# Key chunks of P.V in pairs in TensorE's order, in a fused attention and mixture-of-experts kernel

## What is computed

```python
q, k, v = (jnp.einsum('bsd,hdk->bhsk', x, w) for w in (w_q, w_k, w_v))   # x: 8 x 512 x 128, 16 heads of 64
weights = jax.nn.softmax(jnp.einsum('bhqk,bhmk->bhqm', q, k) / 8, axis=-1)
z = jnp.einsum('bhqm,bhmk->bhqk', weights, v)
z = jnp.einsum('bse,ed->bsd', jnp.transpose(z, (0, 2, 1, 3)).reshape(b, s, h * dk), w_o)
x = layernorm(x + (x + z))
combine = ...          # softmax over the top 2 of 8 experts of x @ gate_w, 0 for the others
h = jax.nn.silu(jnp.einsum('bsd,edf->ebsf', x, w1))
y = jnp.einsum('ebsf,efd->ebsd', h, w2)
x = layernorm(x + (x + jnp.einsum('ebsd,bse->bsd', y, combine)))
```

## Time and profile before

| | |
|---|---|
| median of 3 runs | 1282.63 us (1282.48 to 1285.91) |
| span of the profiled execution, first to last instruction | 1280.0 us |
| its own time: span and 2.6 us around it, by the median | about 1282.6 us |
| PE busy | 1196.7 us, 93% |
| DVE busy | 987.7 us, 77% |
| POOL, ACT busy | 679.6 us (53%), 602.0 us (47%) |

### The profile page before, as it was taken

How to read it: one execution, slowest core, us unless ns; L and a number is a source line. 1 busy time by engine, 2 the same in 40 slices (tenths; PEclk the granted TensorE clock), 3 DMA queues, 4 the chain that set the end, 5 groups by cost and what they waited for, 6 DMA issues and landing times. The chain is left out here.

```text
span 1280.0 us, 20247 instructions
## 1 busy us (share of the span) xinstructions
PE 1196.7 (93%) x4952; PEld 693.9 (54%) x4952; DVE 987.7 (77%) x1618; ACT 602.0 (47%) x744; POOL 679.6 (53%) x502
## 2 busy tenths in 40 slices
PE   5799999999999999999999999999998788888886
PEld 3454555555555555555555555555553566666664
DVE  4586888788888788888788888788887667777764
ACT  4444444444444444444444444444443555556553
POOL 0464644455544455544555544555546366666665
PEclk9898999999999999999999999999999889999999
DMA  9666666566665565665666665656660000000000
GB/s 213 162 161 153 157 155 157 144 156 147 157 156 140 144 155 146 158 159 153 150 150 153 159 148 140 150 149 152 160 161 21 21 9 17 17 17 16 8 9 17
DMA packets 91643, 153.47 MB, mean 120 GB/s; under 512 B 18016, under 2 KB 36960, under 8 KB 91616
## 3 DMA queue, kind: packets, MB, share of 16 engines
q1 hardware_dynamic: 91616, 153.14, 48.1%
HBM read 6.30 MB, written 2.10 MB: 7 GB/s over the span
## 5 line engine op out<-in xcount | busy, mean ns | idle before, releaser
L1025 DVE TENSOR_REDUCE neg_max<-psum 128x1 fp32r<-128x512 f32 x512 | 345.1, 680 | 114.1 <-PE psum L530 112.1
L1040 DVE RECIPROCAL zT<-zT 128x128 f32<-128x128 f32 x256 | 241.4, 944 | 4.2 <-ACT zT L865 2.2
L530 PE MATMUL psum<-k_stack,q_stack 128*128 128x512 f32 x512 | 224.6, 451 | 6.8 <-DVE neg_max L1025 1.4
L555 PE MATMUL psum<-q_stack,k_stack 128*128 128x512 f32 x512 | 210.5, 411 | 9.9 <-DMA q_stack<-q_stack 7.4
L858 ACT ACTIVATE probs_even<-psum 128x1024 f32<-128x1024 f32 x128 | 131.0, 1023 | 179.1 <-PE psum L556 179.1
L556 PE MATMUL psum<-q_stack,k_stack 65*128 65x512 f32 x512 | 205.2, 401 | 0.0
L396 POOL TENSOR_TENSOR probs_sum<-probs_even 128x512 f32<-128x512 f32 x64 | 82.5, 1289 | 227.4 <-PE psum L581 187.2
L396 POOL TENSOR_TENSOR probs_sum<-x_tok 128x512 f32<-128x512 f32 x64 | 82.2, 1284 | 226.9 <-PE psum L581 226.9
L530 PEld LDWEIGHTS psum<-k_stack,q_stack 128*128 128x128 f32 x512 | 97.1, 190 | 185.0 <-DVE neg_max L1025 87.9
L396 POOL TENSOR_TENSOR probs_sum<-probs_sum,probs_even 128x512 f32<-128x512 f32 x128 | 164.1, 1282 | 14.5 <-ACT probs_even L858 3.3
L396 POOL TENSOR_TENSOR probs_sum<-probs_sum,x_tok 128x512 f32<-128x512 f32 x128 | 164.3, 1283 | 11.3
(11 more groups left out here) (119 smaller groups left out, 1927.1 us busy)
## 6 DMA issues: line engine op xcount, KB each, us to landing
q_stack<-q_pair SPq DMA_DIRECT2D x128, 256.0 KB, 3.0
k_stack<-k_pair SPq DMA_DIRECT2D x128, 256.0 KB, 3.6
q_stack<-q_pair SPq DMA_DIRECT2D x128, 128.0 KB, 3.5
k_stack<-k_pair SPq DMA_DIRECT2D x128, 128.0 KB, 3.4
xT_cur<-xT SPq DMA_DIRECT2D x32, 512.0 KB, 3.0
wqk_cur<-w_tab SPq DMA_DIRECT2D x63, 256.0 KB, 3.3
wo_cur<-w_tab SPq DMA_DIRECT2D x64, 128.0 KB, 3.0
x_tok<-L_attn_x_dram SPq DMA_DIRECT2D x8, 256.0 KB, 5.4
```

Of the source, the lines that this page charges most:

```text
L530: nc.tensor.matmul(psum[:, COARSE + t % 2, :], q_stack[j][:, h, 0, t * P:(t + 1) * P], k_stack[j][:, h, 0, :], start=True, stop=True).then ...
L555: nc.tensor.matmul(psum[:, t, :], k_stack[j][:, h, 0, keys], q_stack[j][:, h, 0, :], start=True, stop=False)
L1025: nc.vector.tensor_reduce(neg_max[h][:, t:t + 1], psum[:, COARSE + t % 2, :], AX.X, ALU.max, negate=True).then_inc(s["max_done"], 1)
L1040: nc.vector.reciprocal(zT[:, cols], zT[:, cols]).then_inc(s["r_done"], 1)
```

## The change

In TensorE's body, P.V chunk 0 moves behind coarse 0.2, so that chunks 0 and 1 stand next to each other, and chunk 2 moves from its place ahead of `project_out` to a place behind coarse 1.2, next to chunk 3. No instruction is added or removed, and the programs of the other engines keep their order.

```diff
@@ -638,10 +638,9 @@
                 if project:
                     project_q(n + 2, turn(n + 2, j), j)
                 next_coarse(0, 1)
+                next_coarse(0, 2)
                 if former:
                     times_v(n - 1, 1 - j, 0)
-                next_coarse(0, 2)
-                if former:
                     times_v(n - 1, 1 - j, 1)
                     sum_probs(n - 1, 1 - j)
                 next_coarse(0, 3)
@@ -652,8 +651,6 @@
                     project_k(n + 2, j)
                 scores(n, j, 1, (1,))
                 next_coarse(1, 0)
-                if former:
-                    times_v(n - 1, 1 - j, 2)
                 if before_former:
                     project_out(n - 2)
                 next_coarse(1, 1)
@@ -661,6 +658,7 @@
                     project_v(n)
                 next_coarse(1, 2)
                 if former:
+                    times_v(n - 1, 1 - j, 2)
                     times_v(n - 1, 1 - j, 3)
                 next_coarse(1, 3)
```

## The result

The changed kernel takes 1294.16 us (median of 4 runs, 1291.27 to 1296.73), the kernel before 1283.15 (4 runs, 1282.48 to 1285.91): 1.0087 of it, 95% interval 1.0067 to 1.0107. It is 11.0 us slower. The forecast was 1303 in a range of 1291 to 1312, slower with 0.86. The direction and the mechanism were right; the size was nearly twice what it should have been.

What follows compares the result with a forecast made beforehand. TensorE's order was taken to bound the kernel. The loop's +18.6, unrolled bodies' +2.9 and -1.0 for bodies 1, 62 and 63 gave +20.5 on a span of 1280.0, plus 2.6 around it: 1303 us, range 1291 to 1312.

Steps and rivals of the forecast that it cites:

- What bounds it: Steady loop: TensorE's order sets the time, busy 15.28 and 14.02 us of bodies of 15.28 and 14.19.
- Price of an excursion: TensorE between coarse tiles: one excursion into P.V less is worth 0.35 us; the change takes away two per body.
- First half: Coarse 0.2 ahead of chunk 0 waits for maximum 0.0: 0.05 us lost in the even body, 0.14 gained in the odd.
- the sequencer's preparation of P.V: First half, even body: steps ahead of P.V now follow coarse 0.2, so P.V starts 0.53 us behind it.
- Second half: Without chunk 2, TensorE idles for K ahead of `project_out`: 0.59 us lost in the even body, 0.19 in the odd.
- The jump is covered: End of odd body: the sequencer jumps during the two chunks; next scores follow coarse 1.3 by 0.34 us instead of 0.60.
- Sum: Two bodies lose 0.69 us, 27 loop passes 18.6; with the other bodies, 20.5 on the span of 1280.0.
- The unrolled bodies: Bodies 2 to 7, where nothing jumps: three times (0.05 + 0.59) and three times (0.45 - 0.14), +2.9 us.
- The rest: Bodies 62 and 63 project no K, so lack its wait: some gain, -1.0 us together with body 1.
- the uncovered jump: Rival, end of odd body: the jump stays uncovered, 7 us more, 1310; chance 0.15.
- The full pay of the first half: Rival: coarse 0.2 is not late, 0.35 us gained in each body, 1285, no change; chance 0.06.
- The gain of both excursions in each body: Rival: neither wait shows, each body wins 2 x 0.35 us, 1240; faster had chance 0.08.

Runs made afterwards that it cites:

- e4: Kernel before with coarse 0.2 ahead of chunk 0 and, in even bodies, chunks 2 and 3 both ahead of `project_out`: 1277.49 us, 0.9971 of before.
- e1: Kernel before with only the first half of the change, coarse 0.2 ahead of chunk 0: 1275.74 us, 0.9962 of before.
- e6: Kernel before with coarse 0.2 ahead of chunk 0, coarse 1.0 and 1.1, then chunks 2 and 3, ahead of `project_out`, VectorE reordered: 1245.24 us, 0.9713.
- e2: Kernel before with only the second half of the change, chunks 2 and 3 together behind coarse 1.2: 1300.42 us, 1.0149 of before.
- e5: Changed kernel with K of pair n+2 and maximum 1.0 ahead of the second reciprocal on VectorE: 1293.21 us, 1.0084 of before.
- e3: Changed kernel with coarse 1.1 moved ahead of `project_out`: 1281.37 us, 0.9999 of before.
- e7: e4 with VectorE's fourth reciprocal of even bodies straight behind the third, ahead of the accumulation: 1261.11 us, 0.9846 of before.

## Why the prediction was right, and where its size was off

- **What bounds it**: right. TensorE's order set the time; VectorE's programs were the same, and its busy time in two bodies hardly moved (24.22 to 24.21).
- **Price of an excursion**, 0.35: right, 0.34 in e4. It was the smaller cost here: the chunk had been the cover for a wait. What makes the price, no run shows: P.V differs from the tiles around it in its output columns (64 against 128) and in its data type (float32 against fp32r), and nothing separates the two.
- **First half**: the wait of coarse 0.2 came at its place. Even body: 0.05 lost was forecast, 0.07 gained is there (3.72 to 3.65). **This step failed**: "the sequencer's preparation of P.V ... now it follows coarse 0.2. So P.V starts at about 605.89 + 0.53". P.V starts 0.43 behind the tile. The same 0.43 is there without the preparation: chunk 1, which has no such steps, stood 0.43 behind coarse 0.2 before the change (606.80 to 607.23), and in the odd body it is 0.43 too (626.22 to 626.65). So the preparation costs nothing that shows. The 0.53 isn't what the rows give either: 605.3 to 605.79 is 0.5. Odd body: 0.14 forecast, 0.16 in e1.
- **Second half**: the hole ended 0.25 behind K's end, 0.22 forecast, and the idle time in it is 0.68, about 0.8 forecast. The 0.22 came near with some luck: its 0.12 for one step of the sequencer is a quarter of the 0.5 that the first half got wrong. In the changed profile L590 and L591 are at 617.7 and 617.8, printed to a tenth, which doesn't settle it. Coarse 1.3 in the even body 0.57 late, 0.59 forecast; in the odd body 4.28 against 3.84 from coarse 1.0 on, 0.44 late, 0.45 forecast. The jump is covered, 0.26 back, as forecast. A further 0.09 was missed: the scores behind an uncovered jump took 1.97 to the next transpose (631.92 to 633.89); now it is 1.88 (637.08 to 638.96). The first of those matmuls makes the difference: the second followed it by 0.33 (631.92 to 632.25), and now by 0.24 (637.08 to 637.32).
- **Sum**: 0.69 forecast for two bodies, 0.42 measured. Of the difference of 0.27 the even first half makes 0.12 and the scores behind the jump 0.09; the rest is several of 0.01 to 0.02. The band of 1295 to 1309 is narrower than its own rule: 0.1 at four starts a pass would be 11 us either way in the loop.
- **The unrolled bodies**: +2.9 forecast, and the stretch to body 8 is 0.7 shorter. Body 3 grew by 0.41 (13.70 to 14.11, below), where 0.31 was forecast for an odd one: the 0.45 was counted from a coarse 1.3 that comes later in the loop than here. Body 4 shrank from 20.92 to 19.14 us, with a mean clock of 0.84 before and 0.91 after:

```profile
96.56:117.48 20.92, 18.47 (x68) 10.21 (x67) 13.04 (x20) 7.80 (x11) 9.22 (x8) 0.84 0.70 183
```

```profile
96.79:115.93 19.14, 16.50 (x69) 9.84 (x68) 12.38 (x19) 7.71 (x11) 8.83 (x7) 0.91 0.73 192
```

Nothing ties this to the change: in the nine profiles body 4 takes 20.7 to 20.9 us with 0.84 (before, e4, e6), 18.8 to 19.5 with 0.91 (the changed kernel, e1, e2, e5) and 17.4 to 17.9 with 1.00 (e3, e7), and e4 and e7 have the same order on TensorE. What sets it stays open.
- **The rest**, from body 61 on, is 2.2 us longer, where a gain was put in for the last bodies. Bodies 61 and 62 make 0.3 of it. The other 1.9 lie behind them, mostly in the experts; that stretch takes 308.1 us before, 310.0 in the changed kernel, and 308.4 to 310.1 in the seven others, so no effect of the change can be read from it.
- **Luck**: the forecast was more than 3 us too high ahead of body 8 and about 3 too low in the rest, and the two cancel. The loop makes the miss: 18.6 forecast, 10.6 measured.
- **The rivals**: the uncovered jump fell (0.34), though e5 shows that it returns with a late maximum. The full pay of the first half fell in e1. The gain of both excursions in each body, 1240, did not come with this order: the weight load of coarse 0.2 idles 0.46 for the maximum and TensorE 0.68 for K. In e6 two excursions less in each body, and the waits that went with them, are worth 37 us.

What was not tried is to take the wait for K away altogether, with another bank than MISC for `project_out`; in MISC it would write over K.

## What to carry to other kernels

Before moving work out of a gap between two others, look at the wait behind it: work that looks like an interruption can be the cover for a hand-over, and moving it away can cost more than the interruption, as in e2, where two bodies lost 0.63. To save the interruption, bring the other piece to the cover, not the cover to the other piece; then follow the freed time to the next wait, which may be one instruction in another engine's order. Compare the release of the wait with the time at which the engine would be there without the cover: here both numbers were in the trace before the change.

## What the runs showed of the hardware that was not expected

The loop's jump on TensorE cost 0.35 us a pass before the change and 0.40 in e5, where the sequencer came to it only when coarse 1.3 started (631.4 against 631.32; 638.2 against 638.06). It cost nothing that shows in the changed kernel, where it came 0.6 ahead of that tile (636.1 against 636.74). Before the change an odd body takes 14.19 us in the loop, and in its unrolled form, body 3, 13.70:

```profile
82.86:96.56 13.70, 13.70 (x56) 7.10 (x55) 11.86 (x19) 6.42 (x9) 8.59 (x7) 1.00 0.54 125
```

After the change, with the jump covered, the same unrolled body takes as long as the odd one in the loop (14.11):

```profile
82.68:96.79 14.11, 13.42 (x56) 7.21 (x55) 12.09 (x19) 6.42 (x9) 8.85 (x7) 1.00 0.56 131
```

Of the 0.49 between the two forms before the change, 0.26 lie between the last coarse tile and the next scores and 0.09 in those scores; these 0.35 are the jump's. In e5, where coarse 1.3 was not late, the same two are 0.31 and 0.09. The remaining 0.14 lie ahead of the last coarse tile and are not the jump's: in the loop VectorE's accumulation (L1061), behind which maximum 1.1 stands, starts 1.18 behind `project_out` (628.80 to 629.98), and in the unrolled body 1.01. Why, no run shows.

```profile
629.98 0.69 DVE L1061 TENSOR_TENSOR acc<-psum,acc 128x512 f32 x1 [0.21 <-PE psum L480]
```

```profile
91.97 0.50 PE L478 MATMUL psum<-zT_hi,wo_cur 128*128 128x512 f32 x1
...
92.98 0.69 DVE L1061 TENSOR_TENSOR acc<-psum,acc 128x512 f32<-128x512 f32 x1
```

So a loss in an unrolled odd body of 0.41 turned into a gain of 0.08 in the looped one.
